# Three of the four additions to x moved from VectorE to ScalarE and GpSimd, a wider bias matmul, and a new order of the work, the fill above all

## The chip, the cores and the metric

The kernel runs on one core of a Trainium2 chip. The metric is the device time of one execution in microseconds (us). Engines are named as in the profile: PE is TensorE's matmuls, PEld its weight loads, DVE is VectorE, ACT is ScalarE, POOL is GpSimd, SP is SyncE, which here issues every DMA.

## The reference

The input x is 16 batches of 256 rows by 256 channels. Each batch goes through four blocks, one after the other, and each adds to x:

```
m = silu(cond) @ w_ada + b_ada                       # nine shifts, scales and gates
x += g_msa * (self_attention(ln(x)*(1+sc)+sh) @ w_so + b_so)     # windows of 128 rows, rolled by 64
x += g_mca * (topk_cross_attention(ln(x).., ctx) @ w_co + b_co)  # softmax over the 16 largest scores of 256
x += g_mlp * ((silu(a) * b) @ w_m2 + b_m2)                       # a, b = h @ w_m1 + b_m1, 2 x 1024 wide
x += attention(ada_ln(x), ada_ln(ctx)) @ Wp + bp                 # second layer, 256 rows against 256
```

All attentions have 16 heads of depth 16. The context is (16, 256, 256) as well.

## The kernel before, in words

A batch is two tiles of 128 rows, side by side in one SBUF tile of 128 x 512 float32 (X, eight of them in turn). Each batch passes four stages, named by a letter: w (window attention), t (top-k attention), m (the gated layer), l (the last attention). Float32 products are made of three float16 matmuls: every operand is split into a high part (ACT, "sp" for activations, "wh" for weights) and a low part (POOL, "lo"; DVE, "wl" for weights).

The work is cut into pieces, such as `xt_w:0`, and each engine runs its pieces in a fixed order, one batch interleaved with others. The order comes from tables of due times written out in the file (WINDOW, TOP, MIDDLE, LAST, WEIGHTS, a start for each batch and stage, and SHIFTS, one offset for each piece of each batch); `orders` sorts by them (line 541). Only the order counts: the engines wait for semaphores and never for a time. Both versions have the same PE and SP pieces.

The pieces that this text speaks of, with their lines:

- `xi` (L896): SP loads x of a batch by three DMAs. `wd` (L891): SP loads one of 22 weight pieces (numbers 0 to 21 in the order of `weight_chunks`) into a staging buffer; the first seven have a buffer of their own, and later ones wait until the piece three before has been split (`wl`). `wh` (ACT, L1195) and `wl` (DVE, L1335) split a piece; `wp` (PE) multiplies a piece of the modulation weights with cond, 16 or 8 matmuls, and its `wl` (L1340) adds the bias.
- `bn` (DVE, L1375) statistics of a normalization, `rs` (POOL, L1463 to L1471) normalizes, `x4` (PE) turns the result, `sp` (ACT) applies scale and shift and splits it, `lo` (POOL, L1478) makes the low part, `pj` (PE) projects to q or k, 12 matmuls, `vj` to v. `in` (SP, L916) copies q or k into stacks, six DMAs.
- `a` (PE) scores; `rm` (DVE, L1386) row maxima in stages w and l; `t1`, `t2` (DVE, L1396 to L1413) the top 16 in stage t, and `fx` (POOL) after them; `gd`, `gc`, `gg` carry the maxima back into the stack; `b` turned scores, `e` (ACT) exp, `o` (PE) attended, `os` (ACT) its copy.
- `ot` (PE), `nv` (DVE, L1427, L1431), `bk` (PE), `sp`, `lo`, `pr` (PE) end a block: normalize, turn, project. `fo` (ACT, L1266) applies gate and bias into a "full" tile (three in turn, shared with `sp`), `xt` (PE) turns that back to rows in PSUM, and `xa` (DVE, L1439) adds it to X. In stage l there is no gate: `pr_l` writes rows, its bias comes by one matmul of 33 rows (`ones`, `last_bias`: row 0 has the high part, row 32 the low part, the others are zero), and `xa_l` adds the bank.
- Three PSUM banks ("work") are taken in turn by x4, pj, vj, gd, ot, bk, pr, xt, m1, m2 and wp. Before it writes, PE waits for whoever reads the bank's previous content (`d_freed`).
- `IDLE_WORK` names PE pieces ahead of which PE first runs a number of matmuls without use on the identity, 821 in all.

Of the kernel before, what the change touches and what calls it, by code (L numbers as in the profile page):

```python
# [34 lines left out]
def by_depth(a, n):  # L35
# [11 lines left out]
    ("sp", "xi:0@-149.05811 in_wq:0@-22.39374 in_wk:0@-21.63518 gg_w:0@-6.70743 gg_w:1@-6.20742 gg_w:2@3.72515 "  # L47
            "gg_w:3@10.37658"),
    ("pe", "x4_n1:0@-6.90706 pj_wq:0@-2.39993 pj_wk:0@4.1906 vj_w:0@6.71658 a_w:0@26.64525 a_w:1@29.95151 "
            "gd_w:0@32.06858 a_w:2@32.07884 gd_w:1@32.31761 gd_w:2@34.56035 a_w:3@38.24856 b_w:0@38.32788 "  # L50
            "o_w:0@40.56372 gd_w:3@41.01137 b_w:1@43.06835 b_w:2@45.03826 o_w:1@46.42386 o_w:2@48.26397 "
            "b_w:3@49.43673 o_w:3@51.60005 ot_w:0@54.39099 bk_w:0@56.76485 pr_w:0@60.86232 xt_w:0@64.09604"),
    ("act", "sp_n1:0@-5.60821 sp_wq:0@0.69514 sp_wk:0@4.47055 v_w:0@8.07868 gc_w:0@31.57295 gc_w:1@35.50605 "
            "gc_w:2@38.34758 e_w:0@41.65703 gc_w:3@43.05115 os_w:0@43.2033 e_w:1@43.93529 e_w:2@46.48944 "
            "os_w:1@48.5639 os_w:2@52.23033 e_w:3@52.69148 os_w:3@54.20941 sp_ws:0@58.10794 fo_w:0@63.30753"),
    ("dve", "bn_n1:0@-17.84269 rm_w:0@24.47919 rm_w:1@26.55546 rm_w:2@29.71092 rm_w:3@39.32701 nv_w:0@54.92831 "
            "xa_w:0@62.38605"),
    ("pool", "rs_n1:0@-19.44322 lo_n1:0@-8.8718 lo_wq:0@3.49632 lo_wk:0@11.63506 lo_ws:0@54.42283"),
# [3 lines left out]
    ("sp", "ct:0@-99.73834 in_tk:0@-44.57923 in_tq:0@-23.93763 gg_t:0@11.55535 gg_t:1@18.98072 gg_t:2@33.72058 "  # L62
            "gg_t:3@44.28659"),
    ("pe", "pj_tk:0@-7.66208 x4_n2:0@1.34278 pj_tq:0@10.7192 a_t:0@24.62457 a_t:1@36.3855 a_t:2@40.46992 "
            "gd_t:0@41.16911 b_t:0@46.39389 a_t:3@47.54705 b_t:1@49.06852 vj_t:0@49.42558 gd_t:1@52.91429 "
            "a_t:4@53.28068 b_t:2@59.66427 a_t:5@60.56827 o_t:0@62.91677 a_t:6@66.51438 b_t:3@67.69902 "
            "gd_t:2@68.67071 o_t:1@76.5107 b_t:4@79.63426 a_t:7@80.32481 gd_t:3@82.46194 b_t:5@83.04624 "
            "o_t:2@85.87755 b_t:6@86.53666 b_t:7@89.11422 o_t:3@92.86888"),
    ("act", "sp_cx:0@-11.9872 sp_tk:0@-5.86499 sp_n2:0@2.28585 sp_tq:0@12.69497 gc_t:0@44.9994 e_t:0@47.48754 "
            "v_t:0@51.05134 gc_t:1@53.3508 e_t:1@55.62168 e_t:2@59.98971 os_t:0@63.8611 gc_t:2@69.69816 "  # L70
            "e_t:3@71.71361 e_t:4@79.20016 os_t:1@79.33838 gc_t:3@82.25219 e_t:5@82.98353 os_t:2@87.13718 "
            "e_t:6@89.31508 e_t:7@91.75307 os_t:3@95.36907"),
    ("dve", "bn_n2:0@-3.74256 t1:0@24.82785 t1:1@25.99561 t2:0@26.02817 t2:1@30.1113 t1:2@38.51452 t1:3@39.55482 "
            "t2:2@41.13393 t2:3@41.34036 t1:4@41.52443 t1:5@45.44448 t2:4@46.78488 t2:5@47.10927 t1:6@47.16237 "
            "t1:7@48.39117 t2:6@51.57509 t2:7@52.32364 t1:8@52.56969 t1:9@54.60461 t2:8@55.29963 t2:9@60.52053 "
            "t1:10@61.06788 t1:11@62.9661 t2:10@63.3474 t2:11@66.8321 t1:12@68.23409 t1:13@68.4942 t2:12@71.10979 "
            "t2:13@74.68463 t1:14@74.98922 t1:15@75.34729 t2:14@76.80089 t2:15@80.70227"),
    ("pool", "lo_cx:0@-11.37668 lo_tk:0@-4.00308 rs_n2:0@-2.79057 lo_n2:0@5.12064 lo_tq:0@11.96397 fx:0@32.9126 "
            "fx:1@32.92828 fx:2@34.80931 fx:3@34.93037 fx:4@42.97415 fx:5@50.16423 fx:6@55.57803 fx:7@58.79649 "
            "fx:8@60.94042 fx:9@64.73968 fx:10@69.85252 fx:11@73.33177 fx:12@82.59758 fx:13@84.73536 "  # L80
            "fx:14@87.7392 fx:15@88.83329"),
# [6 lines left out]
    ("act", "sp_ts:0@25.62374 fo_t:0@31.51421 sp_n3:0@39.79357 mt:0@48.14528 mt:1@50.27942 mh:0@57.14955 "
            "mh:1@59.59317 mt:2@63.96734 mt:3@68.23663 mh:2@72.50858 mh:3@73.50494 fo_m:0@82.75238"),
    ("dve", "nv_t:0@22.38771 xa_t:0@31.54577 bn_n3:0@33.90082 xa_m:0@86.06433"),  # L90
    ("pool", "lo_ts:0@18.5931 rs_n3:0@30.90423 lo_n3:0@43.18365 mp:0@52.38292 mp:1@55.13443 ml:0@55.70021 "
            "ml:1@62.11994 mp:2@65.96046 mp:3@75.67304 ml:2@75.96474 ml:3@79.05536"),
# [11 lines left out]
    ("act", "sp_nc:0@-13.51752 sp_n4:0@15.92879 sp_lk:0@22.52586 sp_lq:0@23.83301 gc_l:0@45.50798 v_l:0@45.67024 "
            "e_l:0@52.82507 e_l:1@54.70265 gc_l:1@55.69581 os_l:0@59.35014 gc_l:2@67.94285 e_l:2@69.03957 "
            "e_l:3@75.1829 os_l:1@78.73982 e_l:4@81.89438 e_l:5@87.37575 gc_l:3@87.96386 e_l:6@100.22673 "
            "os_l:2@101.30232 e_l:7@105.8488 os_l:3@113.77208 sp_ls:0@120.4135"),
    ("dve", "bn_nc:0@-63.04501 bn_n4:0@11.41235 rm_l:0@34.11091 rm_l:1@40.7024 rm_l:2@46.39432 rm_l:3@46.6088 "
            "rm_l:4@48.85676 rm_l:5@50.04474 rm_l:6@69.12191 rm_l:7@77.58587 nv_l:0@113.53821 xa_l:0@125.89374"),
# [4 lines left out]
WEIGHTS = (
    ("sp", "wd:0@-820.48184 wd:1@-815.84396 wd:2@-760.47169 wd:3@-638.08125 wd:4@-637.89492 wd:5@-572.64794 "
            "wd:6@-562.34813 wd:7@-554.80374 wd:8@-514.06737 wd:9@-477.63975 wd:10@-468.27362 wd:11@-444.59686 "
            "wd:12@-392.89263 wd:13@-361.08397 wd:14@-349.29088 wd:15@-341.82081 wd:16@-334.33457 "
            "wd:17@-214.76897 wd:18@-178.65186 wd:19@-104.2353 wd:20@-38.57571 wd:21@-35.09744"),
    ("pe", "wp:0@-826.19586 wp:4@-619.28852 wp:6@-565.62339 wp:9@-443.02674 wp:14@-319.17591 wp:17@-89.17967 "
            "wp:19@-81.40903"),  # L120
    ("act", "wh:1@-800.15056 wh:2@-725.47492 wh:3@-631.48284 wh:5@-568.06825 wh:7@-547.52076 wh:8@-506.16029 "
            "wh:10@-466.20739 wh:11@-446.42844 wh:12@-394.66871 wh:13@-366.17785 wh:15@-351.03887 "
            "wh:16@-111.90745 wh:18@-62.30983 wh:20@-27.42181 wh:21@-8.30481"),
    ("dve", "wl:0@-820.27463 wl:1@-752.90035 wl:2@-722.26279 wl:3@-623.49788 wl:4@-614.54744 wl:5@-574.94317 "
            "wl:6@-553.38003 wl:7@-542.07996 wl:8@-460.25079 wl:9@-447.93484 wl:10@-445.85958 wl:11@-433.74773 "
            "wl:12@-347.43476 wl:13@-339.36652 wl:14@-91.58312 wl:15@-59.93139 wl:16@-38.46673 wl:17@-34.65238 "
            "wl:18@-32.21702 wl:19@-12.98123 wl:20@16.52988 wl:21@58.21069"),
)
# [1399 lines left out]
```

## Time and profile before

| | us |
|---|---|
| median of three runs | 1345.95 |
| lowest, highest | 1345.39, 1347.81 |
| the profiled execution | 1343.52 |
| its span, first to last instruction | 1341.7 |
| busy in it: PE, DVE, ACT, POOL | 1233.3, 1146.4, 994.8, 875.2 |

The span is cut in the text into the fill (up to 105 us, where the first top-k begins), a ramp (to 305), the steady part (to 1078, twelve batches of 64 us), the run-out (to 1222) and the drain. Instructions pass each engine in order, so a busy share near 1 over hundreds of microseconds means that this engine leaves no room. A matmul's recorded duration overlaps the next one's, so the pitch of matmuls is less than their mean duration. "PEclk" is the clock granted to PE, 1 being 2.4 GHz and 0.5 being 1.2 GHz.

### The profile page before, as it was taken

What the parts mean: (1) busy time and instruction counts of PE and PEld (TensorE: products, weight loads), DVE (VectorE), ACT (ScalarE), POOL (GpSimd) and SP (SyncE); (2) the same over time, 40 slices, a digit from 0 to 9 for tenths busy, and PEclk for the clock granted to TensorE, in tenths of its full rate; (3) what the DMA queues carried; (4) which work ended last, traced back from release to release, by engine and by line L of the source; (5) the groups of instructions that cost most, each with busy time, mean ns of one, the idle gap of its engine ahead of it and who ended that gap; (6) DMA issues with size and microseconds to landing.
All of it is one profiled execution on the core that took longest, in us unless ns stands there. A gap on an engine that the chain in (4) does not pass through costs nothing. (4 is left out here: it accounts for less than half of the span.)

```text
span 1341.7 us, 39506 instructions
## 1 busy us (share of the span) xinstructions
PE 1233.3 (92%) x14013; PEld 874.8 (65%) x14013; DVE 1146.4 (85%) x3819; ACT 994.8 (74%) x2001; POOL 875.2 (65%) x1161
## 2 busy tenths in 40 slices
PE   6678789989999999999999999999999999989887
PEld 6566466656666676767676766666666756656654
DVE  4418999989999999999999999999999999896322
ACT  3343577869888787979797979888787968776743
POOL 0132468867868586869586876868685857666630
PEclk9888999989999999999999999999999999999998
DMA  6420202121213031212122121213020211110010
GB/s 209 140 55 20 64 22 53 37 61 26 73 26 80 9 80 29 66 32 61 45 53 53 33 66 26 65 38 82 16 73 14 59 47 42 26 31 20 25 33 17
DMA packets 111392, 67.28 MB, mean 50 GB/s; under 512 B 13836, under 2 KB 107870, under 8 KB 111198
## 3 DMA queue, kind: packets, MB, share of 16 engines
q1 hardware_dynamic: 111198, 64.76, 17.9%
...
## 5 line engine op out<-in xcount | busy, mean ns | idle before, releaser
L1248 ACT ACTIVATE prob<-turned_score 128x1024 f32<-128x1024 f32 x320 | 326.4, 1020 | 108.7 <-PE turned_score L947 102.9
L1478 POOL TENSOR_TENSOR pair<-full,pair 128x512 f16<-128x512 f32 x192 | 221.0, 1160 | 140.7 <-ACT pair L1222 137.2
L1484 POOL TENSOR_SCALAR far<-far 128x512 bf16<-128x512 bf16 x256 | 158.0, 617 | 77.2 <-DVE far L1413 57.7
L1386 DVE TENSOR_REDUCE rowmax_l<-score 128x4 f32<-128x1024 f32 x128 | 156.0, 1219 | 61.2 <-PE score L947 50.3
L1399 DVE MATCH_REPLACE8 rest<-top,score 128x256 f32<-128x256 f32 x512 | 208.2, 415 | 0.0
L1413 DVE MATCH_REPLACE8 far<-best,rest 128x256 bf16<-128x256 f32 x512 | 205.5, 409 | 0.0
L1396 DVE MAX8 top<-score 128x8 f32<-128x256 f32 x512 | 192.7, 418 | 4.9 <-PE score L947 4.8
L947 PE MATMUL work<-pair_n,w_m_hi 128*128 128x256 f16 x1024 | 172.8, 273 | 1.5 <-issue 1.4
L947 PE MATMUL work<-pair_n,w_m_lo 128*128 128x256 f16 x512 | 139.6, 273 | 0.0
L1463 POOL TENSOR_SCALAR rstd_n<-mean_var_n 128x2 f32<-128x2 f32 x64 | 12.6, 197 | 190.2 <-DVE mean_var_n L1378 187.2
L1222 ACT ACTIVATE pair<-full 128x512 f16<-128x512 f32 x192 | 121.0, 630 | 19.0 <-DMA q_stack_l<-pair 1.0
L947 PEld LDWEIGHTS work<-pair_n,w_m_hi 128*128 128x128 f16 x1024 | 95.6, 98 | 23.3 <-issue 10.4
L1386 DVE TENSOR_REDUCE rowmax_w<-score 128x8 f32<-128x1024 f32 x64 | 78.0, 1219 | 36.7 <-PE score L947 19.7
L1406 DVE MAX8 best<-rest 128x8 f32<-128x256 f32 x256 | 106.7, 417 | 0.0
L1408 DVE MAX8 best<-rest 128x8 f32<-128x256 f32 x256 | 104.7, 409 | 0.0
L947 PE MATMUL work<-hid,w_m_hi 128*128 128x256 f16 x512 | 86.9, 273 | 0.5 <-POOL hid L1497 0.4
L1493 POOL TENSOR_TENSOR gated<-gated,linear 128x512 f32<-128x512 f32 x64 | 81.4, 1272 | 5.0
L1490 POOL TENSOR_TENSOR linear<-linear,other 128x512 f32<-128x512 f32 x64 | 81.4, 1272 | 0.0
L1497 POOL TENSOR_TENSOR hid<-gated,hid 128x512 f16<-128x512 f32 x64 | 74.1, 1158 | 10.4 <-ACT hid L1291 5.2
L947 PE MATMUL turned_score<-ident,far 128*128 128x128 bf16 x1024 | 80.8, 223 | 0.0
L947 PEld LDWEIGHTS turned_score<-ident,far 128*128 128x128 bf16 x1024 | 58.6, 99 | 27.8 <-issue 26.0
L1439 DVE TENSOR_TENSOR x_tile<-x_tile,work 128x512 f32<-128x512 f32 x64 | 43.5, 679 | 36.7 <-PE work L944 27.9
...
## 6 DMA issues: line engine op xcount, KB each, us to landing
...
```

The source lines that it names most:

```text
L947: return pe.matmul(o, lhsT, rhs, start=start, stop=stop)
L1222: act.activation(pair_tile(s, b)[:, 0, :, :], tile[:, :, :], ACT.Copy).then_inc(split_hi, 1)
L1248: act.activation(prob[:, at:at + 2, :], both_b[:, :, :], ACT.Exp).then_inc(exp_done, 1)
L1386: dve.tensor_reduce(rowmax[s][n % 2][:, :].rearrange("p (z m) -> p z m", z=2)[:, :, at:at + wide], both_a[:, :, :].rearrange("p z (h k) -> ...
L1396: first = [step(dve.max(eight[:, t, :], bank[:, t * L:(t + 1) * L])) for t in range(LT)]
L1399: m = dve.match_replace(rest[p % 2][:, t, :], eight[:, t, :], bank[:, t * L:(t + 1) * L], -FAR)
L1406: second = [step(dve.max(best[p % 2][:, 0, :], rest[p % 2][:, 0, :]))]
L1408: second.append(step(dve.max(best[p % 2][:, 1, :], rest[p % 2][:, 1, :])))
L1413: m = dve.match_replace(far[p % NFAR][:, t, :], best[p % 2][:, t, :], rest[p % 2][:, t, :], -FAR)
L1478: pool.tensor_tensor(pr[:, 1, :, :], whole[:, :, :], pr[:, 0, :, :], ALU.subtract).then_inc(split_lo, 1)
L1484: pool.tensor_scalar(tile, tile, FAR, -1.0, ALU.add, ALU.mult).then_inc(far_fixed, 1)
L1490: pool.tensor_tensor(linear[:, two, :], linear[:, two, :], other[:, two, :], ALU.mult).then_inc(pair_product, 1)
```

## The change

In stages w, t and m, DVE's `xa` is replaced by two pieces: `xe` (ACT) copies the turned bank into the full tile that `fo` had written, and `xp` (POOL) adds that tile to X. The bank is free for PE after `xe`; the full tile is free for ACT after `xp`; the next normalization waits for `xp`. `xa_l` stays on DVE.

```diff
@@ build @@
-        ones = sb("ones", [33, L], F16)
-        last_bias = sb("last_bias", [33, C], F16)
+        ones = sb("ones", [P, L], F16)
+        last_bias = sb("last_bias", [P, C], F16)
+        x_moved = {s: sem(f"x_moved_{s}") for s in "wtm"}
@@ d_freed, full_freed @@
             if kind == "xt":
-                return x_added[s], b + 1
+                return x_moved[s], b + 1
...
-            return d_ready, d_no["xt_" + s, key[1], 0]
+            return x_added[s], key[1] + 1
@@ scalar @@
+                elif kind == "xe":
+                    act.wait_ge(d_ready, d_no["xt_" + s, b, 0])
+                    act.activation(full_tile("fo_" + s, b)[:, :, :],
+                                   d_bank("xt_" + s, b, 0)[:, :].rearrange("p (t c) -> p t c", t=LT),
+                                   ACT.Copy).then_inc(x_moved[s], 1)
@@ vector @@
                 elif kind == "xa":
-                    src = "pr_l" if s == "l" else "xt_" + s
-                    dve.wait_ge(d_ready, d_no[src, b, 0])
+                    dve.wait_ge(d_ready, d_no["pr_l", b, 0])
@@ gpsimd @@
+                elif kind == "xp":
+                    pool.wait_ge(x_moved[s], b + 1)
+                    x = X[b % NX]
+                    pool.tensor_tensor(x[:, :, :], x[:, :, :], full_tile("fo_" + s, b)[:, :, :],
+                                       ALU.add).then_inc(x_added[s], 1)
```

All tables of due times are new, and with them the order on every engine. The matmuls without use are 590 instead of 821. The beginning of each queue, as it follows from the tables (a number after the colon is the batch, for wd, wp, wh and wl the piece of weights):

```
SP before   wd0-13 xi:0 wd14-18 xi:1 wd19 in_wq:0 in_wk:0 wd20 wd21 xi:2 ct:0 gg_w:0 (4) xi:3 in_wq:1 in_tk:0 in_wk:1 in_tq:0
SP after    wd0-6 xi:0 wd7-10 xi:1 in_wq:0 in_wk:0 wd11 gg_w:0 ct:0 wd12 gg_w:0 wd13 gg_w:0 wd14 gg_w:0 wd15 xi:2
            wd16-18 in_wk:1 wd19 in_wq:1 wd20 wd21 in_tk:0 in_tq:0
PE before   wp0 4 6 9 14 x4_n1:0 pj_wq:0 pj_wk:0 wp17 wp19 a_w:0 vj_w:0 gd_w:0 ... bk_w:0 pj_tk:0 pj_wq:1 pr_w:0 xt_w:0
            pj_wk:1 vj_w:1 x4_n2:0 pj_tq:0 a_w:1
PE after    wp0 4 x4_n1:0 wp6 pj_wq:0 vj_w:0 pj_wk:0 wp9 a_w:0 gd_w:0 ... pj_wq:1 bk_w:0 wp14 pr_w:0 pj_wk:1 vj_w:1
            xt_w:0 pj_tk:0 wp17 x4_n2:0 pj_tq:0 a_w:1 wp19
DVE before  wl0-13 bn_n1:0 wl14-18 rm_w:0 wl19 ... xa_w:0 bn_n2:0 wl21 rm_w:1 rm_w:1 bn_n1:2 rm_w:1 t1:0
DVE after   wl0 bn_n1:0 wl1-9 bn_n1:1 wl10 rm_w:0 (3) wl11 rm_w:0 wl12 nv_w:0 wl13 wl14 bn_n1:2 wl15 bn_n2:0 wl16-18
            rm_w:1 wl19 rm_w:1 wl20 rm_w:1 wl21 t1:0
```

From the third batch on the orders differ by neighbours that change places. Near the end, DVE's `nv_t:15` stood behind `xa_m:14` and `bn_n4:14` and now stands ahead of `bn_n4:14`. In the steady part three to five ACT pieces lie between `fo` and its `xe`, and four to seven between `xe_w` or `xe_t` and the next piece that writes the same full tile.

## Rows read from the trace of the kernel before

**Rows 1.** Busy time of each engine in five stretches of the span.
```profile
0.00:105.00 105.00, 76.03 (x822) 68.01 (x824) 35.79 (x71) 38.13 (x65) 20.49 (x35) 0.89 0.43 132
105.00:305.00 200.00, 169.73 (x1951) 119.40 (x1953) 187.96 (x686) 130.92 (x265) 124.67 (x168) 0.94 0.16 41
305.00:1078.00 773.00, 757.65 (x8735) 530.33 (x8723) 749.24 (x2536) 653.52 (x1334) 587.41 (x779) 1.00 0.19 49
1078.00:1222.00 144.00, 129.44 (x1433) 87.50 (x1436) 134.27 (x459) 105.86 (x215) 96.04 (x124) 0.99 0.12 30
1222.00:1342.00 120.00, 100.44 (x1095) 69.53 (x1083) 39.11 (x72) 66.34 (x125) 46.57 (x56) 0.96 0.10 26
```
In each: start and end, length, busy PE, PEld, DVE, ACT, POOL (instructions), PEclk, DMA share, GB/s.

**Rows 2.** Groups by form, whole span, PE: the matmuls without use.
```profile
L947 PE MATMUL attended<-ident 128*128 128x128 bf16 x821 | 58.1, 234 | 4.6 <-ACT osum_t L1253 3.2 <-ACT osum_l L1253 1.4
```

**Rows 3.** Timeline of SP, the fill.
```profile
8.34 0.47 SPq L891 DMA_DIRECT2D prob<-in_L_xcond_w_ada  x1
...
28.70 1.71 SPq L896 DMA_DIRECT2D x_tile<-in_x  x3
...
46.40 3.87 SPq L916 DMA_DIRECT2D q_stack_w<-pair  x6
...
96.20 3.75 SPq L916 DMA_DIRECT2D q_stack_t<-pair  x6
```

**Rows 4.** Timeline of ACT, the fill: the split that waited for wd:5.
```profile
14.87 1.06 ACT L1195 ACTIVATE w_kv_hi<-prob 128x1024 f16<-128x1024 f32 x1 [2.08 <-DMA prob<-in_L_xcond_w_kv]
```

**Rows 5.** Timeline of DVE, the fill: bn_n1:0, xa_w:0 and the first t1.
```profile
34.56 0.75 DVE L1375 BATCH_NORM_STATS2 stats_n<-x_tile 128x6 f32<-128x256 f32 x2
...
83.39 0.69 DVE L1439 TENSOR_TENSOR x_tile<-x_tile,work 128x512 f32<-128x512 f32 x1 [7.18 <-PE work L944]
...
105.33 0.76 DVE L1396 MAX8 top<-score 128x8 f32<-128x256 f32 x2 [1.06 <-PE score L947]
```

**Rows 6.** Timeline of PE, the fill: wp:9, a_w:0, gd_w:0 and a_t:0.
```profile
20.41 3.57 PE L947 MATMUL work<-cond_T,gated 128*128 128x16 f32 x16
...
55.97 0.61 PE L947 MATMUL score<-k_stack_w,q_stack_w 48*128 48x128 f16 x8 [6.50 <-DMA k_stack_w<-pair]
...
58.99 0.27 PE L944 MATMUL work<-ident,rowmax_w 128*8 128x128 f32 x1
...
104.90 0.39 PE L947 MATMUL score<-k_stack_t,q_stack_t 48*128 48x256 f16 x4
```

**Rows 7.** Groups by form, 305 to 1078 us: DVE, POOL, ACT.
```profile
L1439 DVE TENSOR_TENSOR x_tile<-x_tile,work 128x512 f32<-128x512 f32 x42 | 28.4, 677 | 0.0
...
L1490 POOL TENSOR_TENSOR linear<-linear,other 128x512 f32<-128x512 f32 x43 | 54.7, 1273 | 0.0
...
L1229 ACT ACTIVATE v_w<-work 128x512 f32<-128x512 f32 x11 | 6.8, 614 | 0.5
```

**Rows 8.** Groups by form, 105 to 1222 us, DVE.
```profile
L1439 DVE TENSOR_TENSOR x_tile<-x_tile,work 128x512 f32<-128x512 f32 x56 | 38.0, 678 | 3.0 <-PE work L944 3.0
```

**Rows 9.** The chain that ended last, in order of time, the drain.
```profile
1235.05 0.70 DVE x_tile L1439
...
1236.66 0.35 DVE recip L1427
...
1261.91 2.62 PE work L947 x24
...
1284.35 0.70 DVE x_tile L1439
```

**Rows 10.** Timelines of POOL and DVE, 46 to 59 us.
```profile
46.54 1.16 POOL L1478 TENSOR_TENSOR pair<-full,pair 128x512 f16<-128x512 f32 x1 [0.23 <-ACT pair L1222]
...
46.84 0.90 DVE L1345 TENSOR_SCALAR sskv<-sskv 128x32 f32<-128x32 f32 x1
...
58.07 0.18 DVE L1345 TENSOR_SCALAR ssq<-ssq 128x32 f32<-128x32 f32 x1
```

**Rows 11.** Instructions of the tile last_bias.
```profile
L947 PE MATMUL work<-last_bias,ones x32: 279/280/281, 362.2 to 1337.3; 33*128 33x256 f16 x32
```

More of the change, by code:

```diff
@@ L46 @@
 WINDOW = (
[L47 to L58, printed above, removed]
+    ("sp", "xi:0@-140.59579 in_wq:0@-44.62479 in_wk:0@-35.05263 gg_w:0@-10.09389 gg_w:1@-7.96093 gg_w:2@-6.73594 "
+            "gg_w:3@-5.61648"),
@@ new lines @@
+    ("pe", "x4_n1:0@-5.24861 pj_wq:0@-1.82554 pj_wk:0@2.56111 vj_w:0@8.8856 a_w:0@27.15713 gd_w:0@28.71315 "
+            "a_w:1@28.91227 a_w:2@30.1969 gd_w:1@32.76704 gd_w:2@33.60692 b_w:0@35.74671 a_w:3@38.1077 "
+            "o_w:0@40.22703 b_w:1@40.45058 gd_w:3@41.80271 b_w:2@44.42801 o_w:1@44.96523 o_w:2@46.88591 "
+            "b_w:3@48.58494 o_w:3@52.11361 ot_w:0@53.95135 bk_w:0@56.50117 pr_w:0@61.43494 xt_w:0@62.8127"),
+    ("act", "sp_n1:0@-4.06447 sp_wq:0@0.49421 sp_wk:0@8.61433 v_w:0@10.70609 gc_w:0@31.83417 gc_w:1@37.15986 "
+            "gc_w:2@38.29682 e_w:0@39.82435 os_w:0@43.98055 e_w:1@44.0931 e_w:2@46.47485 gc_w:3@47.16729 "
+            "os_w:1@47.49739 os_w:2@49.5692 e_w:3@51.20697 os_w:3@53.85179 sp_ws:0@56.56703 fo_w:0@62.13315 "
+            "xe_w:0@65.95909"),
@@ L59 @@
+    ("dve", "bn_n1:0@-32.83897 rm_w:0@26.67262 rm_w:1@27.48801 rm_w:2@29.65466 rm_w:3@39.90605 nv_w:0@53.42126"),
+    ("pool", "rs_n1:0@-18.2856 lo_n1:0@-4.88234 lo_wq:0@6.81155 lo_wk:0@16.54635 lo_ws:0@57.58024 xp_w:0@70.30693"),
 )
 TOP = (
[L62 to L81, printed above, removed]
+    ("sp", "ct:0@-83.73655 in_tk:0@-49.67057 in_tq:0@-31.67185 gg_t:0@-9.84262 gg_t:1@8.93994 gg_t:2@16.49826 "
+            "gg_t:3@31.69368"),
@@ L88 @@
[L88 to L92, printed above, removed]
+    ("pe", "ot_t:0@20.21686 bk_t:0@23.47827 pr_t:0@27.716 xt_t:0@31.30999 x4_n3:0@39.51006 m1:0@45.36278 "
+            "m1:1@45.96191 m1:2@50.31727 m1:3@50.39566 m1:4@59.54839 m1:5@60.13659 m1:6@68.47961 m1:7@68.97396 "
+            "m2:0@75.77506 m2:1@75.86697 m2:2@78.69259 m2:3@79.7671 xt_m:0@81.40143"),
@@ new lines @@
+    ("act", "sp_ts:0@25.61449 fo_t:0@30.20828 xe_t:0@32.85826 sp_n3:0@40.84137 mt:0@50.4312 mt:1@53.50237 "
+            "mh:0@58.40605 mt:2@62.75423 mh:1@67.43982 mh:2@69.4835 mt:3@70.37853 mh:3@77.23782 fo_m:0@82.19014 "
+            "xe_m:0@86.38001"),
+    ("dve", "nv_t:0@20.57952 bn_n3:0@32.36206"),
+    ("pool", "lo_ts:0@25.52856 xp_t:0@34.24957 rs_n3:0@35.51024 lo_n3:0@41.87616 mp:0@57.1406 mp:1@59.18956 "
+            "ml:0@62.91446 mp:2@74.81297 ml:1@75.71887 ml:2@77.87228 mp:3@82.19988 ml:3@83.85812 xp_m:0@86.72378"),
@@ L104 @@
[L104 to L109, printed above, removed]
@@ L112 @@
+    ("pool", "rs_nc:0@-32.96239 lo_nc:0@-3.73687 rs_n4:0@11.15526 lo_n4:0@18.02354 lo_lk:0@22.99294 "
+            "lo_lq:0@23.79888 lo_ls:0@129.45719"),
 )
 WEIGHTS = (
[L115 to L118, printed above, removed]
@@ L169, in starts @@
-    last = (151.36396, 215.22396, 279.12744, 343.10857, 407.08958, 471.11544, 535.15606, 599.23103,
-            663.1372, 727.04507, 790.95327, 855.07932, 919.14649, 983.11864, 1047.0723, 1116.04643)
+    window = (-67.17447, -9.93588, 55.56255, 119.68295, 183.52807, 247.32902, 311.36813, 375.26229,
+              439.23743, 503.19103, 567.08786, 630.91978, 694.56229, 758.91638, 822.50679, 886.55299)
+    top = (0.4062, 63.78711, 127.9181, 191.79986, 255.86254, 319.8805, 383.85617, 447.64115, 511.71497,
+           575.52217, 639.48353, 703.4377, 767.27941, 831.36669, 895.20594, 958.79828)
@@ L522, in shifts @@
     return found
-IDLE_WORK = ("wp:0:14=119 x4_n1:0:0=24 pj_wq:0:0=45 wp:0:19=21 a_w:0:2=21 bk_w:0:0=18 pr_w:0:0=7 xt_w:0:0=17 "
-             "x4_n2:0:0=24 pj_tq:0:0=45 a_w:1:0=30 a_w:1:2=21 a_t:0:0=31 a_w:1:3=20 bk_w:1:0=25 pr_w:1:0=43 "
-             "a_t:0:4=10 a_t:0:7=25 a_t:1:0=7 bk_t:15:0=10 x4_n4:14:0=15 xt_t:15:0=17 a_l:14:3=15 bk_l:13:0=8 "
-             "xt_m:15:0=17 x4_n4:15:0=34 pj_lq:15:0=17 a_l:15:0=26 bk_l:14:0=8 a_l:15:3=9 a_l:15:7=14 "
-             "o_l:15:3=17 bk_l:15:0=18 pr_l:15:0=43")
+IDLE_WORK = ("a_w:0:0=60 pr_w:0:0=11 pj_tq:0:0=45 a_w:1:2=22 a_t:0:0=21 o_w:1:0=19 bk_w:1:0=20 pr_w:1:0=8 "
+             "xt_w:1:0=14 x4_n2:1:0=22 pj_tq:1:0=12 a_w:2:1=28 a_t:1:0=13 a_t:1:3=21 x4_n3:0:0=11 pr_w:2:0=8 "
+             "pj_wq:3:0=7 o_l:13:1=12 x4_n3:15:0=31 a_l:14:3=15 ot_l:13:0=6 bk_l:13:0=8 xt_m:15:0=17 "
+             "a_l:15:0=17 a_l:15:1=21 a_l:15:3=21 a_l:15:4=6 a_l:15:5=9 o_l:15:0=7 o_l:15:3=17 bk_l:15:0=18 "
+             "pr_l:15:0=43")
 def idle_work():
```

756 lines of the change are left out of this document (390 added, 366 removed).

## The prediction, made before the changed kernel ran

> **What bounds the kernel now.** I read the busy times by stretch first. In the steady part PE is busy for 757.7 of 773 us and DVE for 749.2, so both are nearly full and neither hides the other; ACT (653.5) and POOL (587.4) have room [rows 1]. PE could gain at most 773 - 757.7 = 15.4 us there. In the ramp DVE is the fuller one, 188.0 of 200 against 169.7, and also in the run-out, 134.3 of 144 against 129.4. In the fill nothing is full: PE is busy for 76 of 105 us, much of that with matmuls without use (58.1 us for 821 over the run, 71 ns each [rows 2]), DVE for 36. The fill is one long chain of waits for batch 0. The drain is such a chain again, with PE busy for 100 of 120 us.
>
> PE's useful work is the same in both versions. So the time falls by what PE stops idling (or spending without use), and only by that.
>
> The second view is the timeline of the fill, engine by engine. The reader is to see that x of batch 0 was asked for at 28.7 us, behind fourteen pieces of weights [rows 3]; that its statistics began at 34.56 [rows 5]; that its first scores came at 55.97 and the first scores of stage t at 104.9 [rows 6]; and that DVE, which from there on has almost no gap, began its top-k at 105.33 [rows 5].
>
> **The fill, part by part.** (a) x first. The seven weight pieces that need no wait stay ahead; SP issues the last of them at 8.34 and is free at 8.81 [rows 3]. The three DMAs of x take 1.71 us to issue, so they are out at 10.5. How late they land is read from the piece two places ahead of them: it was issued just before 8.34 and ACT, waiting for it, began at 14.87 [rows 4], some 7 us after. One more piece of 512 KB and x's 256 KB lie behind it, so x lands at 16.5 to 17.5; I take 17.0. DVE has only wl:0 ahead. bn_n1:0 starts 17.5 us earlier than 34.56.
>
> (b) To the first scores. From bn_n1:0 to a_w:0 it was 55.97 - 34.56 = 21.4 us. New in that path are wp:6 ahead of pj_wq:0 and vj_w:0 ahead of pj_wk:0. wp's 16 matmuls take 3.57 us [rows 6], but PE waits there anyway for ACT's and POOL's splitting (POOL's part alone 1.16 us [rows 10]); between 0 and 3.6, I take 0.8. vj_w is 12 matmuls: 1.3 us at the full clock (half of 2.62 for 24 [rows 9]), 2.4 at the low one (58.99 - 56.58, the gap that it filled behind a_w:0 [rows 6]). It delays k only, whose six DMAs stand behind 3.87 us of q's [rows 3]; between 0 and 2.4, I take 1.4, which holds also that the projections have fewer warming matmuls ahead. Together +2.2: a_w:0 at 17.0 + 21.4 + 2.2 = 40.6, which is 15.4 earlier.
>
> (c) To the first top-k it was 105.33 - 55.97 = 49.4 us. With vj_w:0 gone from between a_w:0 and gd_w:0 the maxima go back about 1.1 earlier. The addition w:0 becomes longer: an ACT copy of 128x512 out of PSUM takes 0.61 and a POOL addition of two such float32 tiles 1.27, against 0.68 on DVE [rows 7], with one more handover between engines of under 0.1: +1.25. PE now runs pj_wk:1 and vj_w:1 (2.62 us) between pr_w:0 and xt_w:0, where fo_w hides some 1.2: +1.4. The splits of pieces 11 to 21 (ACT and DVE, up to some 1.2 each) and the loads behind them now stand between the steps of batches 0 and 1, and SP's in_tq:0, issued at 96.2 before [rows 3], stands behind wd:19 to 21, which wait for wl:16 to 18, which stand behind bn_n2:0. Walking these queues by the durations above I find each piece there in time or late by tenths; DVE is idle for two thirds of the fill [rows 1]. Between 0 and +6, I take +0.7. Ten matmuls without use fewer ahead of a_t:0: -0.7. Sum -1.1 + 1.25 + 1.4 + 0.7 - 0.7 = +1.55, so t1:0 at 40.6 + 49.4 + 1.5 = 91.5 against 105.3: **-13.8 us**. By then PE has done the same pieces as before, so the whole train behind starts that much earlier.
>
> **The additions.** DVE loses 56 additions of 678 ns between 105 and 1222 us [rows 8], less the 14 of stage l, which stay. I cost by stretch. Ramp: DVE is the fuller engine, and seven additions, 4.8 us with stage l's, lie in it; between 0 and -4.8, I take -3.3. Steady part: three quarters of 28.4 us [rows 7], 21.3, leave DVE, but PE has only 15.4 to gain, and the order there hardly changes; what PE waits is partly for DVE's reading of scores, partly none of DVE's. Between -13 and +10 (below), I take -3. Run-out: seven additions again and PE idle for 14.6 of 144; between 0 and -4, I take -3. On the other side ACT gains 3 x 0.61 = 1.8 us a batch, POOL 3 x 1.27 = 3.8, on 54 and 49 of 64: room remains. The full tile is held for some two microseconds longer, but four to seven ACT pieces of 0.3 to 1.6 us lie between xe and its next writer. The cover is thin where POOL's queue is long.
>
> **The drain.** Three of the shortened additions lie in the chain, at 1235.05, one at 1244.8 and at 1284.35 [rows 9]: 3 x 1.25 = +3.75. nv_t:15 no longer stands behind xa_m:14 and bn_n4:14: it started at 1236.66, 1.6 us after that addition began; -1.6. The rest of the new order near the end I take at 0, between -3 and +3. Sum **+2**.
>
> **The bias matmuls** took 280 ns at 33 rows [rows 11]; the row count is the depth of the product and not the columns that stream. Between -0.1 and +0.1 us each for 32, half of it hidden; I take 0.
>
> **The sum** for the profiled execution: 1343.5 - 13.8 - 3.3 - 3 - 3 + 2 = 1322.4. It lay 2.4 below the median of the runs shown, so the forecast for the median is 1324.8.
>
> **A rule of the skill against the change.** DVE's tensor_scalar of 32 columns took 0.90 us at 46.84 and ended at 47.74, just when POOL's splitting ended (47.70); the same instruction took 0.18 at 58.07, with POOL idle [rows 10]. The Trainium skill (SBUF — State Buffer, "Who interferes with whom") says that GpSimd has no SBUF port of its own: a VectorE instruction in a two-port mode, or with two SBUF inputs while GpSimd reads, is locked out until the other is done. By that rule the trace agrees here. Perfetto Trace Analysis, "Optimizing Scalar/DVE Operations", adds that work moved between these two may not help. In the steady part the additions of POOL's kind show a mean of 1273 ns with DVE 97% busy [rows 7], so the lock seldom bites; in the fill eleven weight splits on DVE have two SBUF inputs and now run beside POOL's work, which by the rule would cost up to some 3 us more than my +0.7.
>
> **Rivals.**
> 1. The fill gives half. The new queue of SP and the late splits delay in_tq:0 or t1:0 by the 6 us of the upper bound, and ramp and steady part give nothing for DVE's relief, since PE is full: -13.8 + 6 + 2 = -6 in the profiled execution, with a microsecond or two either way 1337 to 1340. For it: nine pieces of weights wait for each other through three buffers. Against: DVE and ACT are mostly idle then.
> 2. DVE was the true bound. Then ramp and run-out give 4.8 and 4, the steady part 13 of PE's 15.4: -13.8 - 4.8 - 13 - 4 + 2 = -33.6, 1312. For it: DVE is at 97% and PE's scores wait for its reads. Against: PE at 98% would have to reach nearly 100%.
> 3. Slower. The detour of an addition over ACT and POOL ends as PE's wait: PE needs the bank, or ACT the full tile, or x4 the next normalization, before POOL, which works in lumps of over 3 us in stage m, has added. The place is xe and xp of the 42 x 3/4 = 32 additions of the steady part and the 10 of ramp and run-out. The price is up to 1.25 us each if nothing covers it, 52 us; break-even is where it costs 20/42 = 0.5 us each. At 0.8 us: 34 - 14 + 2 = +22 less the little of DVE, and the time 1365. Against: PE's order has several pieces between pr and xt and between xt and the next x4.
> 4. No change: what comes early in the fill is lost before the steady part, since another wait, such as the last weights for stage m, sets its start. The m weights are needed only after stage t of batch 0, far behind 105 us, so this is unlikely; 1346.
>
> **How the numbers follow.** Forecast 0.50, its own range 1317 to 1333. Rival 1 0.23, rival 2 0.12, rival 3 0.10, rival 4 0.05. The range of eight in ten goes from 1310, just below rival 2, to 1341, above rival 1, and leaves out rivals 3 and 4 and the far end of rival 2. Within 0.2% (2.7 us, what a measurement can tell from no change) lies most of rival 4: 0.04. Faster: 0.50 + 0.23 + 0.12 = 0.85. Slower: 0.11.
>
> **What would show it.** In the changed trace: bn_n1:0 at 17, a_w:0 near 40.6, the first MAX8 near 91.5, the last t2:15 near 1222 - 23 = 1199. PE's steady share 98% or more at the same 64 us a batch, DVE's about 94%. xe of 0.6 and xp of 1.27 us. If PE's waits for POOL or ACT grow by more than half a microsecond an addition, rival 3 is right; if the batch takes 63 us, rival 2. A first MAX8 later than 97 makes the fill's step wrong.

## The result, and the profile after

| | kernel before | changed kernel |
|---|---|---|
| median (lowest to highest), us | 1346.9 (1345.4 to 1348.2) | 1330.7 (1329.3 to 1331.9) |
| ratio to before, 95% interval | | 0.988 (0.9863 to 0.9897) |
| profiled execution: time, span, us | 1343.5, 1341.7 | 1330.8, 1328.7 |

The change made the kernel 16.2 us faster; 1324.8 was forecast, with 1310 to 1341 as the range. Other kernels of this study ran on other chips or at other times, where the kernel before took 1348 to 1351 us, so they are compared by their ratios (time over that of the kernel before in the same set of runs, with a 95% interval), or by places in their profiles. A profile is one execution: that of before lay 3.4 us below its median, which makes every distance between two profiles smaller than that between the medians.

The busy times of the changed kernel, in stretches that start 14 us earlier than those of before [rows 1] and have the same columns:

```profile
0.00:91.00 91.00, 59.25 (x549) 49.98 (x550) 33.20 (x69) 38.12 (x66) 28.52 (x41) 0.85 0.48 143
91.00:291.00 200.00, 175.25 (x2035) 124.61 (x2032) 185.91 (x685) 136.33 (x274) 132.39 (x172) 0.94 0.17 46
291.00:1064.00 773.00, 751.79 (x8683) 528.95 (x8685) 731.40 (x2501) 662.83 (x1362) 625.34 (x809) 1.00 0.19 49
1064.00:1208.00 144.00, 133.30 (x1469) 89.35 (x1461) 133.95 (x462) 110.70 (x223) 105.85 (x132) 0.98 0.13 33
1208.00:1330.00 122.00, 97.64 (x1059) 68.00 (x1055) 35.55 (x65) 66.76 (x126) 48.92 (x58) 0.94 0.09 23
```

The reader is to see the third line. DVE is busy for 731.4 us, 17.8 less than before; of its additions there, 28.4 us, only stage l's 6.6 are left. But PE is busy for 751.8, not for more than 757.7: it idles for 21.2 us of 773 where it had idled for 15.4. The relief of DVE did not reach PE.

The fill, in lines that answer to [rows 3], [rows 5] and [rows 6], first SP, then DVE, then PE's first scores:

```profile
8.71 1.70 SPq L901 DMA_DIRECT2D x_tile<-in_x  x3
...
84.71 4.63 SPq L921 DMA_DIRECT2D k_stack_t<-pair  x6
89.44 3.75 SPq L921 DMA_DIRECT2D q_stack_t<-pair  x6
```
```profile
17.05 0.75 DVE L1385 BATCH_NORM_STATS2 stats_n<-x_tile 128x6 f32<-128x256 f32 x2 [4.00 <-DMA x_tile<-in_x]
...
42.96 1.23 DVE L1396 TENSOR_REDUCE rowmax_w<-score 128x8 f32<-128x1024 f32 x1 [4.40 <-PE score L952]
...
95.57 0.76 DVE L1406 MAX8 top<-score 128x8 f32<-128x256 f32 x2 [3.38 <-PE score L952]
```
```profile
42.37 0.48 PE L952 MATMUL score<-k_stack_w,q_stack_w 48*128 48x128 f16 x8 [3.56 <-DMA k_stack_w<-pair]
```

x was asked for at 8.71 and its statistics began at 17.05, both as forecast. The first scores (a_w:0) came at 42.4 for 40.6, and the first MAX8 at 95.6, 9.8 us earlier than before and 4.1 later than forecast.

How long a batch takes is read from one instruction that each has, its first rowmax_w on DVE; for batches 5 and 12 these are, before and then changed:

```profile
361.30 1.22 DVE L1386 TENSOR_REDUCE rowmax_w<-score 128x8 f32<-128x1024 f32 x1
...
866.30 1.21 DVE L1386 TENSOR_REDUCE rowmax_w<-score 128x8 f32<-128x1024 f32 x1
```
```profile
346.43 1.21 DVE L1396 TENSOR_REDUCE rowmax_w<-score 128x8 f32<-128x1024 f32 x1
...
855.12 1.22 DVE L1396 TENSOR_REDUCE rowmax_w<-score 128x8 f32<-128x1024 f32 x1
```

Seven batches took 505.0 us before and 508.7 now: 72.1 and 72.7 each. The lead is 14.9 us at batch 5 and 11.2 at batch 12. **A batch takes 72 us, and not the 64 that stand in the prediction**: 64 is the distance in the ticks of the tables, which are no microseconds. The steady stretch holds 10.7 batches, not 12, as the 42 additions in it [rows 7], four a batch, could have told. No term of the sum was taken from it, but "on 54 and 49 of 64" is wrong: ACT and POOL are busy for 61 and 55 us of 72.

At the last t2:15 the lead is 14.7 us (the last MATCH_REPLACE8 of batch 15, before and changed):

```profile
1228.04 0.41 DVE L1413 MATCH_REPLACE8 far<-best,rest 128x256 bf16<-128x256 f32 x1
```
```profile
1213.39 0.41 DVE L1423 MATCH_REPLACE8 far<-best,rest 128x256 bf16<-128x256 f32 x1
```

In the drain an addition of the chain reads as forecast, ACT and POOL where there was one line of 0.70 us [rows 9]:

```profile
1228.24 0.47 PE work L949 x4
1228.73 0.60 ACT full L1276
1229.34 0.07 issue
1229.41 1.27 POOL x_tile L1492
```

It is the only one of its kind in the changed kernel's chain, where three had been counted.

### The profile page after: what moved, and what is told of

Same layout as the page of the kernel before. It is cut to its first block, busy times and chain, and to the rows that moved or that the text cites. A ratio compares the mean times of both kernels' runs of the same rounds, so it can differ in the third digit from the quotient of the medians.

```text
span 1328.7 us, 39097 instructions
## 1 busy us (share of the span) xinstructions
PE 1217.2 (92%) x13782; PEld 860.9 (65%) x13782; DVE 1120.0 (84%) x3777; ACT 1014.7 (76%) x2049; POOL 941.0 (71%) x1209
## 3 DMA queue, kind: packets, MB, share of 16 engines
q1 hardware_dynamic: 111198, 64.76, 18.2%
## 4 chain that ended last, share of the span: by engine, by line
PE 36%; DVE 24%; POOL 6%; issue 5%; SPq 4%; ACT 3%; DMA 2%; DVEq 0%; ACTq 0%; POOLq 0%
PE work L952 17%; PE attended L952 6%; DVE rest L1409 5%; PE work L949 5%; PE turned_score L952 5%; DVE far L1423 5%; DVE top L1406 5%; SPq L921 4%; PE score L952 3%; DVE rowmax_l L1396 3%; DVE best L1416 2%; POOL pair L1487 2%; DVE stats_n L1385 1%; DVE attn L1441 1%; DMA q_stack_t<-pair 1%
## 5 line engine op out<-in xcount | busy, mean ns | idle before, releaser
L1498 POOL TENSOR_SCALAR far<-far 128x512 bf16<-128x512 bf16 x256 | 158.0, 617 | 92.4 <-DVE far L1423 72.9
L1227 ACT ACTIVATE pair<-full 128x512 f16<-128x512 f32 x192 | 120.9, 630 | 17.6 <-ACT full L1220 0.4
L1492 POOL TENSOR_TENSOR x_tile<-x_tile,full 128x512 f32<-128x512 f32 x48 | 61.1, 1273 | 53.1 <-ACT full L1276 46.7
L1480 POOL TENSOR_SCALAR normed<-x_tile,rstd_n 128x256 f32<-128x256 f32 x128 | 71.1, 562 | 7.0
## 6 DMA issues: line engine op xcount, KB each, us to landing
ctx_t<-in_ctx_turned SPq DMA_DIRECT2D x16, 256.0 KB, 2.9
ctx_l<-in_ctx SPq DMA_DIRECT2D x16, 256.0 KB, 2.8
```

The lines of the kernel that those rows point to most:

```text
L1227: act.activation(pair_tile(s, b)[:, 0, :, :], tile[:, :, :], ACT.Copy).then_inc(split_hi, 1)
L1498: pool.tensor_scalar(tile, tile, FAR, -1.0, ALU.add, ALU.mult).then_inc(far_fixed, 1)
```

## The experiments

The orders of the queues come out of tables with some hundreds of numbers, so an edit to one piece alone is made on the list of a queue after the tables have been read. "The orders of before" and "the new orders" are these lists, for all five queues.

**The fill alone.** The kernel before, with the first pieces of each queue in the new order, and with the fill's matmuls without use as in the new order too (557 in all):

```diff
+first = the new orders, up to a_t:0 (PE), t1:0 (DVE), gc_w:1 of batch 0 (ACT), fx:0 (POOL), gg_w:0 of batch 1 (SP)
+plan = {e: first[e] + [k for k in plan[e] if k not in first[e]] for e in plan}
```

> The kernel before, with only the beginning of each queue taken from the new order, up to the first top-k (DVE), the first scores of stage t (PE), the first guard copy of batch 1 (ACT), the first fix of far (POOL) and the first guard DMA of batch 1 (SP); the additions stay on DVE and the rest keeps the old order. Theory A (the gain is the fill's): the first MAX8 comes some 10 us earlier than 105.3, near 94 to 96, and the whole stays ahead by that: 1336 to 1338 against 1347, ratio 0.992. Theory B (the gain is DVE's relief): the early start is lost against a full DVE, under 4 us gained, ratio 0.997 or more.

Measured: 1334.5 us, ratio 0.990 (0.9884 to 0.9917), a little less than the 1336 to 1338 expected. Theory A held: without any addition moved the gain is 13.4 us, where the changed kernel gained 16.2 and, in its repeat below, 18.2. First MAX8 at 94.1; batches of 72.0 us (rowmax_w of batch 5 at 354.7, of batch 12 at 859.0). Between the profiles the lead over the kernel before is 11.2 us at the first MAX8, 6.6 at batch 5 and 9.0 at the end: some of what the fill won was lost in the ramp.

**The additions alone.** The orders of before, with xe and xp put where they stand in the new orders, counted from fo and rs (and the bias over 128 rows):

```diff
-    dve: xa_w, xa_t, xa_m
+    act: xe_* as many pieces behind fo_* as in the new orders
+    pool: xp_* as many pieces ahead of rs_* as in the new orders
```

> The changed code with the old tables: all three additions as ACT copy and GpSimd addition, put into the old order as many pieces after fo and ahead of rs as they have in the new one; fill, weights and matmuls without use as before. Theory A: DVE's relief helps only where DVE is the fuller engine (ramp, run-out), the longer way of an addition takes it back: -4 to +2 us against before. Theory B: 10 to 16 us faster. Theory C (the detour costs in the steady part and the new order only hides it): 3 or more slower.

Measured: 1441.9 us, ratio 1.070 (1.0678 to 1.0716), so Theory C, by far more than its 3 us. Its longest waits from 400 to 1100 us (us in total, times, longest):

```profile
POOL x_tile L1498 <- ACT full L1282: 72.6, 9, 9.7
ACT prob L1259 <- PE turned_score L958: 53.8, 61, 2.3
DVE stats_n L1391 <- POOL x_tile L1498: 39.1, 25, 3.4
```

POOL stands for up to 9.7 us at an addition whose operand ACT has not copied yet, with everything behind it; DVE then waits for POOL. This is rival 3's mechanism at 94 us, some 2 us for each of 48 additions. It is no price of the detour as such: the places were carried over by count and not fitted. It shows that places carried over by count from another order can cost more than all that the change gains.

**The additions back on DVE, all else new.** The three xa of a batch in DVE's queue at the time when the matmuls of xt ended in the changed kernel's profile; xe and xp gone; bias over 33 rows.

```diff
+    dve: xa_w, xa_t, xa_m, each ahead of the first piece begun after its xt had ended
-    act: xe_*        pool: xp_*
```

A first version, with the additions placed by count from bn as in the old orders, gave no time: its queues waited for each other in a ring.

> [...] Theory A (the fill is what was won, the detour over ScalarE and GpSimd is worth nothing or costs a little): 1329 to 1335 us, the steady part back to 72.2 us a batch or equal to the changed kernel's 72.7. Theory B (the rest of the 16 us, some 3, and the steadiness of the middle come from the additions leaving VectorE): 1335 to 1340 us, batches of over 72.9 us. Theory C (the orders fit only the detour, as the additions fit only their own orders): over 1345 us.

Measured: 1352.4 us, ratio 1.0016 (1.0001 to 1.0031), beside the changed kernel unaltered:

> The changed kernel once more, unaltered, as the reference for its neighbours on the same chip. Every theory: 1330 to 1332 us. It is needed because the run with the bias over 33 rows came out 3 us above the changed kernel, in another set of runs.

That one gave 1332.7 us, 0.9861 (0.9838 to 0.9883). So Theory A fell and Theory C held. The fill is as good (first MAX8 at 93.3), but a batch takes 74.2 us:

```profile
350.06 1.21 DVE L1401 TENSOR_REDUCE rowmax_w<-score 128x8 f32<-128x1024 f32 x1
...
869.63 1.21 DVE L1401 TENSOR_REDUCE rowmax_w<-score 128x8 f32<-128x1024 f32 x1
```

What PE waited for longest there, from 291 to 1064 us, is read against the same in the changed kernel and in the kernel before (305 to 1078), in this order:

```profile
PE work L959 <- DVE attn L1446: 17.6, 22, 1.2
PE score L962 <- DVE rest L1414: 4.6, 13, 1.0
PE turned_score L962 <- ACT prob L1263: 4.5, 20, 0.3
PE score L962 <- DVE rowmax_l L1401: 3.2, 15, 0.5
```
```profile
PE work L949 <- DVE attn L1441: 7.2, 18, 0.6
PE turned_score L952 <- ACT prob L1253: 4.3, 19, 0.3
PE attended L952 <- ACT osum_l L1258: 2.4, 10, 0.3
PE score L952 <- DMA q_stack_t<-pair: 2.1, 4, 0.9
```
```profile
PE work L944 <- POOL normed L1471: 6.5, 10, 0.7
PE work L944 <- DVE attn L1431: 2.8, 9, 0.6
```

In the new orders PE stands at the product that DVE's attn feeds: 17.6 us with the additions on DVE, 7.2 without (7.1 with the bias over 33 rows as well). In the old orders that wait was 2.8 with them. So the new orders, as far as tried, need the detour, and the old ones did not. The additions themselves hardly stood waiting where they were put (DVE waited 3.2 us for PE ahead of 42 of them), but one set of places is all that was tried, and a better one isn't ruled out.

**Splits ahead of the statistics.** The changed kernel, with one edit:

```diff
+    dve: wl:1 wl:2 wl:3 wl:5 of batch 0 ahead of bn_n1:0, no longer behind it
```

> The changed kernel with one edit: the four splits of weights that VectorE ran beside GpSimd's first rstd (from 17.9 us) stand ahead of the first statistics, where VectorE idled for 4.0 us. Theory A (the two engines held each other up at the SBUF port: rstd took 4.7 us for 3.2 when undisturbed): rstd_n1 back to 3.2 to 3.4 us, the statistics still at 17.05, everything up to the first MAX8 1.3 to 2 us earlier, total 1329 to 1330. Theory B (GpSimd's first instructions are slow for another reason, such as their first use): rstd_n1 stays at 4.5 us and more, total 1331. Theory C (the splits delay the statistics, since their weights land late): statistics at 18 or later, total 1332.

Measured: 1330.5 us, 0.9845 (0.982 to 0.987); its neighbour, the changed kernel, 0.9861. The ratios don't tell these apart, the profiles do. POOL's first rstd and normed, changed kernel first:

```profile
18.11 1.07 POOL L1472 TENSOR_SCALAR rstd_n<-mean_var_n 128x2 f32<-128x2 f32 x1 [16.23 <-DVE mean_var_n L1388]
19.26 0.52 POOL L1474 TENSOR_SCALAR rstd_n<-mean_var_n 128x2 f32<-128x2 f32 x1
19.75 1.15 POOL L1476 TENSOR_TENSOR rstd_n<-rstd_n,minus_half 128x2 f32<-128x2 f32 x1
21.01 1.78 POOL L1480 TENSOR_SCALAR normed<-x_tile,rstd_n 128x256 f32<-128x256 f32 x2
```
```profile
18.58 0.19 POOL L1487 TENSOR_SCALAR rstd_n<-mean_var_n 128x2 f32<-128x2 f32 x1 [16.70 <-DVE mean_var_n L1403]
18.85 0.19 POOL L1489 TENSOR_SCALAR rstd_n<-mean_var_n 128x2 f32<-128x2 f32 x1
19.01 0.71 POOL L1491 TENSOR_TENSOR rstd_n<-rstd_n,minus_half 128x2 f32<-128x2 f32 x1
19.83 1.09 POOL L1495 TENSOR_SCALAR normed<-x_tile,rstd_n 128x256 f32<-128x256 f32 x2
```

4.7 us became 2.3, by nothing but taking DVE's splits away from beside them. The first of those splits ran from 17.94 to 19.13 in the changed kernel, and POOL's first instruction ended with it:

```profile
17.94 1.19 DVE L1345 TENSOR_TENSOR w_qkv_lo<-hid,w_qkv_hi 128x1024 f16<-128x1024 f32 x1
```

That is Theory A, but its 3.2 us undisturbed was wrong: the kernel before already showed 2.3 for the same instructions (35.62 to 37.95). The first rowmax_w came at 41.15 for 42.96, though the statistics began 0.5 later; the first MAX8 at 93.7, for 95.6 and, in the changed kernel's repeat, 94.4.

**The fill tuned further**, on top of that:

```diff
+    dve: wl:16 and wl:18 behind rm_w:0 and rm_w:1 of batch 1     pool: lo_tk:0 ahead of lo_n2:0
+    sp: in_tk:0, in_tq:0 ahead of wd:19 to wd:21                 pe: wp:19 behind a_t:0, 30 idle matmuls for 45 ahead of pj_tq:0
+    act: wh:20, wh:21 behind gc_w:0 of batch 1
```

> The edit before, and with it what else held the first MAX8 at 95.6 us: the splits beside rstd_n2 moved behind it, the low half of tk ahead of n2's on GpSimd, tk's and tq's transfers ahead of the last three weights on SP's queue, 30 idle matmuls for 45 ahead of pj_tq. Theory A (my missed 4 us are those places): rstd_n2 3.2 us for 4.2, transfers of tk issued at 80 and of tq at 84, first MAX8 at 90.5 to 92, total 1326 to 1328. Theory B (the ramp is bound further on, by the next batch's windows): first MAX8 at 92 or earlier, yet the total within 1 us of the changed kernel's. Theory C (the late weights cost more than they free): over 1332 us.

Measured: 1331.2 us, 0.9854 (0.9832 to 0.9875). rstd and normed of n2 took 2.3 us (72.55 to 74.89) for 4.2 (75.09 to 79.33) in the changed kernel, and the first MAX8 came at 91.4. Yet the last t2 of batch 0 ended at 149.2 for 146.1 with the splits moved alone. The late weights held up the next batch in the ramp; from 90 to 125 us:

```profile
ACT w_Wq_hi L1226 <- DMA hid<-in_L_xcond_Wq: 10.1, 1, 10.1
...
DVE rowmax_w L1422 <- PE score L978: 3.7, 1, 3.7
```

A second try put the weights between the two transfers, and wp:17 behind x4_n2:0:

```diff
+    sp: in_tk:0, wd:19, wd:20, wd:21, in_tq:0      pe: x4_n2:0, wp:17, pj_tq:0 (20 idle matmuls)
+    dve: wl:17, wl:16, wl:18 ahead of rm_w:0 of batch 1
```

> The fill tuned a second time. The last try brought the first MAX8 from 94.4 to 91.4 us and lost it again in the ramp, since the last three weights, put behind tq's transfers, then held up TensorE (the ssq projection waited 1.7 us for its DMA), ScalarE (10.1 us for w_Wq) and VectorE (3.7 us for the scores of the next batch). Now those weights go between tk's and tq's transfers, and the two splits beside rstd_n2 wait for a matmul that stands behind n2's transposes. Theory A (what was lost was those waits): first MAX8 at 90.5 to 92, and the last t2 of batch 0 at 143 to 145 for 146.1 with the splits moved alone; total 1326 to 1329. Theory B (the ramp is bound by the windows of the next batches, not by the first MAX8): last t2 of batch 0 at 146 or later, total 1330 to 1333.

Measured: 1328.5 us, 0.9846 (0.982 to 0.9872), first MAX8 at 93.4, last t2 of batch 0 at 146.8. Neither version can be told from the one edit before them. Both came near their Theory B, in the places more than in the times (the first brought the MAX8 below 92 and gained nothing by it; the second left the last t2 at 146.8, though its time lies in Theory A's range): an earlier first MAX8 alone doesn't shorten the ramp.

**The bias over 33 rows.**

```diff
-ones, last_bias = [P, L], [P, C]
+ones, last_bias = [33, L], [33, C]
```

> The changed kernel with the bias matmuls of 33 rows instead of 128. All theories: the matmul takes 280 ns at either depth and the time is the changed kernel's within 1 us. Rival: a product that leaves three quarters of the array unused lowers the granted clock or slows its neighbours; then this one is slower by a microsecond or more.

> The changed kernel with the bias matmuls over 33 rows again, as in the kernel before. Theory A (rows of zeros cost and bring nothing; the 3 us seen earlier were another chip's spread): a ratio to the kernel before of 0.986 to 0.988, the same as the changed kernel's, and the same waits. Theory B (full rows raise the granted clock or shorten the run-out): a ratio of 0.990, with a lower granted clock after 1208 us than the changed kernel's 0.94.

Measured: 1334.1 and 1334.5 us, 0.990 (0.9881 to 0.9918) and 0.988 (0.9856 to 0.9903), each time about 0.002 above the changed kernel (0.988 and 0.9861), which the intervals can't tell from nothing. The granted clock after 1208 us was 0.90 and 0.93 for 0.94, but these runs are some 7 us behind there and the stretch holds other work, so this decides nothing either. The profile of the weight loads shows where it could come from; before, then changed:

```profile
L947 PEld LDWEIGHTS work<-last_bias,ones 33*128 33x128 f16 x32 | 3.0, 93 | 6.7 <-issue 6.7
```
```profile
L952 PEld LDWEIGHTS work<-last_bias,ones 128*128 128x128 f16 x32 | 3.1, 98 | 0.4
```

Each load of 33 rows had 0.21 us of idle ahead of it, with no wait to explain it; over 128 rows there is none. The batches took 72.9 and 73.0 us with 33 rows, 72.6 to 72.8 in the five runs of new orders with 128. So I put this edit to the kernel before alone:

> The kernel before with one part of the change alone: the bias matmuls over 128 rows. In its trace each weight load of 33 rows came 0.21 us after the engine had gone idle, put down to issue (6.7 us over 32), in the changed kernel 0.4 us over 32. Theory A (in the old orders the stall lies beside VectorE, which sets the batch): 72.1 to 72.2 us a batch as before, a ratio of 0.998 to 1.000. Theory B (TensorE sets the batch, so each stall counts): 71.8 us a batch, 3 to 6 us less, a ratio of 0.995 to 0.998. In both the idle time before the 32 loads falls to under 1 us.

Measured: 1349.5 us, 1.0006 (0.9985 to 1.0028), batches of 72.1, idle ahead of the loads 0.4 us over 32. Theory A: the stall is gone and the batch is no shorter. In the old orders it seems to have lain in time that PE had to spare.

**Both orders in one kernel.** New orders, splits moved, up to a seam; then the orders of before with the additions on DVE:

```diff
+    plan = {e: new[e][:n[e]] + [k for k in old[e] if k not in new[e][:n[e]]] for e in plan}
+    an addition whose xe stands ahead of the seam goes over ACT and POOL, any other is DVE's xa
```

> The changed kernel's queues, with the first splits moved, up to about batch 4 (some 345 us), with ten additions over ScalarE and GpSimd; from there the queues of the kernel before, with the additions on VectorE. Theory A (the new orders win in fill and ramp and give back half a microsecond a batch): 72.1 to 72.2 us a batch after the seam where the changed kernel has 72.7, so that the lead of 16 to 17 us at batch 4 stands at batch 12; total 1326 to 1330. Theory B (the seam costs what the ramp had won, as in the kernel with the new fill alone): a lead of 7 to 10 us from batch 5 on, total 1333 to 1338. Theory C (the half microsecond a batch is not of the orders): over 72.5 us a batch with the old queues too.

> The mixed kernel with its seam some two batches earlier, at about 205 us for 345: new queues and the detour for the fill and the first batches, the old queues and VectorE's additions from there. Theory A (what the ramp won, it won before 205 us, and the old queues keep it): a lead of 15 to 17 us from batch 5 on, 72.2 us a batch, total 1326 to 1329. Theory B (the new order of the ramp up to batch 4 is what keeps the lead; the old ramp loses it, as it did with the new fill alone): a lead of 7 to 12 us from batch 5 on, total 1331 to 1337.

Measured with the seam at some 345 us: 1327.5, 0.9833 (0.9809 to 0.9858). With the seam at some 205 us: 1323.6, 0.9828 (0.9796 to 0.986). The late seam's rowmax_w, then the early one's:

```profile
344.92 1.22 DVE L1420 TENSOR_REDUCE rowmax_w<-score 128x8 f32<-128x1024 f32 x1
...
851.05 1.22 DVE L1420 TENSOR_REDUCE rowmax_w<-score 128x8 f32<-128x1024 f32 x1
```
```profile
345.53 1.22 DVE L1420 TENSOR_REDUCE rowmax_w<-score 128x8 f32<-128x1024 f32 x1
...
851.16 1.21 DVE L1420 TENSOR_REDUCE rowmax_w<-score 128x8 f32<-128x1024 f32 x1
```

72.3 and 72.2 us a batch: Theory A of both (the bias is over 128 rows in both). The lead over the kernel before is 16.4 and 15.8 us at batch 5 and still 15.3 and 15.1 at batch 12, where the changed kernel's had gone from 14.9 to 11.2. The one with the early seam has the lowest median of all that were tried; its interval overlaps those of the splits moved alone and of the changed kernel.

## Why the prediction was right, and where it was off

Measured between the two profiles, with the places named above:

| step | forecast, us | measured, us | read from |
|---|---|---|---|
| fill | -13.8 | -9.8 | first MAX8, 105.33 to 95.57 |
| ramp | -3.3 | -5.1 | lead at batch 5, 14.9 |
| steady part | -3 | +3.7 | lead at batch 12, 11.2 |
| run-out | -3 | -3.5 | last t2:15, lead 14.7 |
| drain | +2 | +1.7 | span, 13.0 |
| sum | -21.1 | -13.0 | |

**The main mechanism was right**: x first shortens the chain of batch 0, and most of what that chain gains arrives at the end. The new fill alone gained 13.4 us. That the total came so near is partly luck: the fill and the steady part together gave 10.7 us less than forecast, ramp, run-out and drain 2.6 more, and 2.4 were kept back for the profile of before.

**The fill was mis-sized by 4.0 us.** The first half, from the statistics to a_w:0, was to take 23.6 us and took 25.3; the second, to t1:0, was to take 50.9 and took 53.2. The step that failed in the first half is part (b), which has no term for DVE's splits beside POOL's normalization: rstd and normed took 4.7 us beside them and 2.3 without, in the run made for it, and with that gone a_w:0 came at 40.43. In the second half the +0.7 of part (c) was too small: the second lock of that kind, at n2, cost 1.9. Together they are as large as the step's miss, and more than the "up to some 3 us" given for the rule. But taking the first away brought the first MAX8 forward by only 0.7 to 1.8 us. With both gone, and some other pieces moved too, it came at 91.4, where the forecast had it; so the locks are shown, and their share in the 4.0 us only roughly. The changed kernel's own repeat had the first MAX8 at 94.4 for 95.6, so a microsecond of this is chance. By that rule (the Trainium skill, SBUF — State Buffer, "Who interferes with whom") a split with two SBUF inputs and POOL's work hold each other up; the trace of the changed kernel agrees (1.07 us for POOL's first instruction beside a split, 0.19 without). I had weighed it and then taken the value without it.

**The steady part had the wrong sign.** I took -3 because DVE lost 21 us of work and PE had 15.4 us to gain. DVE's 17.8 us less was there, but PE's idle time went up by 5.9 us, 0.55 a batch, which is the 72.1 to 72.7. The sentence that failed is "the order there hardly changes". All queues were reordered, and in their new order PE waits 7.2 us for DVE's attn (2.8 before), 4.3 for ACT's prob (0.2) and 2.4 for its osum (0.7); against this only the 6.5 for POOL's normed are gone. The same orders without the detour cost 74.2 us a batch, so the detour is worth 1.5 us a batch in them, less some 0.2 for the 33 rows of that run; the old orders with the additions on DVE cost 72.0 to 72.3 in five kernels. So rival 2's forecast, a steady part 13 us shorter, is refuted: a batch did not get shorter with 17.8 us less on DVE. That DVE's load never matters is not shown; in the new orders it does. What an order made from the old one with a well-placed detour would take was not found; the additions put in by count cost 94 us. The sign "98% or more at the same 64 us" failed too: PE is busy for 97.3% of the stretch.

**Ramp and run-out** came out near the forecast. In the changed kernel the additions and the orders changed together, but the other profiles narrow it down. From the first MAX8 to batch 5 the old orders took 256.0 us, the new fill alone 260.6, and the new orders 256.8 with the additions on DVE; with the detour and the same 33 rows they took 253.5 and 251.7, with 128 rows 250.9 twice. So in these orders some 3 to 5 us of the ramp are the additions', as forecast (-3.3), and the new order alone gives little or nothing there. For the run-out this was not separated. A second profile of nearly the old kernel (the wide bias alone) had its rowmax_w of batch 5 at 367.1, where the old profile has 361.3, and 3.9 of these 5.8 us arose after the first MAX8, so some microseconds of the ramp differ between executions. The -5.1 is uncertain by as much. The sign "last t2:15 near 1199" started from 1222, where the run-out was cut, and not from the last t2:15 at 1228.0; from there the forecast means 1205, and it came at 1213.4.

**Rival 3**, the detour as a wait, was given 0.10. Its mechanism is real (94 us in an order not made for it) but the new orders avoid it: POOL waited for ACT's copies for 17.7 us in the steady part, and no wait of PE for the additions is among its longest. **Rival 1** lay 6 to 9 us above the result: its fill worth half did not come (9.8 of 13.8), but its word that the steady part gives nothing for DVE's relief, since PE is full, did come true. **The drain's** three detours at 1.25 less 1.6 gave +2; measured +1.7. That they agree is in part luck: the chain holds one detour, not three, and from the last t2:15 to the end the new orders took 115.1 us without any detour and 116.8 and 118.3 with it (33 rows in all three), where the old took 113.7. The order, which was to gain 1.6, seems to have cost some 1.4.

**The bias** at 0 was right for the old orders (1.0006, 0.9985 to 1.0028), but its working looked only at the 280 ns of the matmul [rows 11] and not at PEld's idle time in front of its weight load, 6.7 us over 32. In the new orders it may be worth some 0.2 us a batch; that stays open.

**From profile to median** I added 2.4 us, since before's profile lay below its median. That was right to do, for the changed kernel's profile lay on its own median (1330.8 and 1330.7). The five steps gave 8.1 us less than forecast between the spans, 8.4 between the times (1330.8 for 1322.4); 2.4 of this are the profile of before and 0.1 that of the changed kernel, which leaves the 5.9 us between 1324.8 and 1330.7.

**Not tested**: the number of matmuls without use (821 before, 590 changed) went with the order in every version, and the clock granted in the fill was 0.89 before and 0.85 in the changed kernel. What that cost or gave is inside the step of the fill.
